# Cross-attention scores of both query tiles of a head pair in one group of twelve 64-row matmuls

## The chip, the core and the metric

The kernel runs on one core of a Trainium2 chip. The metric is the device time of one execution in microseconds (us). TensorE does the matmuls and transposes, VectorE, ScalarE and GpSimd do the elementwise work, each engine takes its own instructions in the order in which they are written, and semaphores order the engines among each other. The DMA queue of SyncE loads the inputs.

## The reference

A cross-attention layer and a mixture-of-experts layer with its own self-attention, in float32. The change touches the cross-attention alone:

```python
# x: (4, 256, 128), ctx: (4, 512, 256); 16 heads of 64
q = split_heads(layernorm(x) @ Wq) * 64 ** -0.5
k, v = split_heads(ctx @ Wkv)                      # 512 keys, and one learned null key and value per head
k = concat(null_k, k); v = concat(null_v, v)
attn = softmax(q @ k.T, axis=-1)
out = layernorm_affine((attn @ v).merge_heads() @ Wout)
x = x + out
x = x + ffn_block(layernorm(x))                    # self-attention, router, 8 experts, top 2
```

## The kernel before

Float32 products are made from three matmuls each: an operand is split into a high part (`_hi`, a ScalarE copy that rounds) and a low part (`_lo`, VectorE's or GpSimd's difference), and hi*hi, hi*lo and lo*hi are summed in PSUM. The functions `..._head` are ScalarE's copies and `..._tail` VectorE's differences.

`cross_attention` (L317) walks over 32 head pairs `g` (4 batches of 8 pairs, two heads of 64 columns each), with one loop `for s in STEPS` per engine (L547 TensorE, L652 ScalarE, L761 VectorE, L846 GpSimd). The order inside each loop body is written out by hand, and it works on several pairs at once: in step s the scores of pairs s+1 and s+2, the transposes of pair s and one of s-1, the value matmuls of s-1 and s, the q projection of s+2, and the keys and values projections of a pair four ahead (only while such a pair is left). 256 queries make two query tiles t of 128.

For one pair g the way is:
- `project_q`: three matmuls into `unit_bank`; `q_head`, `q_tail` give `q_hi`, `q_lo`.
- `scores(g, t)` (L466): for both heads i the 128 queries of tile t against 512 keys. A head has 64 rows, so the two heads use the upper and the lower 64 rows of the array, and their matmuls run as pairs (the trace shows them as x2): six matmuls per tile, L478. There are four score banks; `score_bank(G, i)` gives tile 0 two of them and tile 1 the other two, for every g. Scores wait until the exponentials of the pair before have read the banks (`p_exp`).
- `maximum` (L709) per tile and head, `shift` (L717) makes the bias, `exponential` (L611) per tile and head with its row sum, `null_gap` (L793) and `null_exponential` (L618) for the null key, `whole_sum` (L802), `inverse_sum` (L724), then GpSimd's `normalise` (L809) per tile and head.
- `transpose_probs(g, i, half)` (L493): four 128x128 transposes, of head i, half of the keys, both query tiles, into `t_bank[half]`; there is one bank per half, so a group waits until `probs_tail` of the group two before has read it (`t_lo_s`). `probs_head` (L627) and `probs_tail` (L733) copy out `pT_hi` and `pT_lo`.
- `weighted_values(g, i)` (L512): eight matmuls into `o_part`, half of `out_bank`; `o_copy` (L636) to `o_raw`, `o_halves` (L743) adds the partitions 0-63 and 64-127 of it into `o_sum`, `o_split` (L837, L839) on GpSimd splits it.
- every fourth step `project_out` (L529) multiplies four pairs by `Wout` into `y_part`, the other half of `out_bank`; `y_copy` (L650, even ones) and `y_add` (L759, odd ones) take it out. `weighted_values(s - 1, 1)` of that step waits for this (L509), since both use the one bank.

`unit_bank` is one bank for q, keys, values and context projections in turn: each waits until the one before has been copied out (`keys_head` L585, `keys_tail` L694, `values_copy` L594, `context_head` L601, `context_tail` L701). In a context step two groups of four transposes of the next batch's context (L82) are added, and one step later the keys projection stands behind the transposes. In a null step (s = 9, 17, 25) two transposes of the null probabilities (L544) are added, and `weighted_values(s, 0)` waits for their split.

Of the kernel before, what the change touches and what calls it, by code (L numbers as in the profile page):

```python
# [20 lines left out]
P = 128  # L21
# [5 lines left out]
QT = N // P  # L27
# [46 lines left out]
HP = H // 2  # L74
# [242 lines left out]
def cross_attention(nc, k, dram):  # L317

    with ExitStack() as ctx:
# [39 lines left out]
        AHEAD = HP // 2  # L359
# [65 lines left out]
        def _(pe):  # L425
# [40 lines left out]
            def scores(g, t):  # L466
                if not 0 <= g < NP:
                    return
                G = 2 * g + t
                if t == 0:  # L470
                    pe.wait_ge(q_lo_s, g + 1)
                    if g >= AHEAD:
                        pe.wait_ge(k_lo_s, g - AHEAD + 1)
                if G >= 2:
                    pe.wait_ge(p_exp, 2 * G - 2)
                for m, (q, keys) in enumerate(((q_hi, k.keys_hi), (q_lo, k.keys_hi), (q_hi, k.keys_lo))):
                    for i in range(2):
                        last = pe.matmul(score_bank(G, i)[:, :], q[rows(i), g % 2, t * P:(t + 1) * P], keys[rows(i), g % HP, :],  # L478
                                         start=m == 0, stop=m == 2)
                        if m == 2:  # L480
                            last.then_inc(s_ps, 1)
# [65 lines left out]
            for s in STEPS:  # L547
                transpose_probs(s - 1, 1, 1)
                if not after_context(s):
                    keys_unit(s)  # L550
                scores(s + 1, 1)
# [3 lines left out]
                if after_context(s):  # L555
                    keys_unit(s)
                    weighted_values(s - 1, 1)
                    values_unit(s)
                else:
                    values_unit(s)  # L560
                    weighted_values(s - 1, 1)
                transpose_probs(s, 1, 0)
                project_q(s + 2)
# [3 lines left out]
                scores(s + 2, 0)  # L567
# [3 lines left out]
        def _(act):  # L571
# [80 lines left out]
            for s in STEPS:  # L652
# [3 lines left out]
                exponential(s + 1, 0, 0)  # L656
                probs_head(s, 0, 0)
                probs_head(s, 0, 1)
                exponential(s + 1, 0, 1)
                y_copy(s)  # L660
                if after_context(s):
                    keys_head(s)
                    o_copy(s - 1, 1)
                    values_copy(s)
                else:
                    values_copy(s)
                    o_copy(s - 1, 1)
                null_exponential(s + 1, 0)
# [3 lines left out]
                null_exponential(s + 1, 1)  # L672
                probs_head(s, 1, 0)
                exponential(s + 1, 1, 0)
                exponential(s + 1, 1, 1)
                o_copy(s, 0)
                context_head(s, 1)

        @block.vector
        def _(dve):  # L680
# [80 lines left out]
            for s in STEPS:  # L761
                probs_tail(s - 1, 1, 1)
# [1038 lines left out]
```

## Time and profile before

| | us |
|---|---|
| median of 3 runs (lowest, highest) | 682.86 (681.18, 684.12) |
| the profiled execution | 680.71 |
| its span, first to last instruction | 678.9 |
| TensorE busy | 580.8 (86%) |
| VectorE busy | 512.8 (76%) |
| ScalarE busy | 423.3 (62%) |
| GpSimd busy | 310.9 (46%) |
| cross-attention steps, 53.15 to 321.44 | 268.29, TensorE busy 258.58 |

The busy shares are means over stages that differ. The last row is the part of the span in which the changed loops run in their full form; it begins with the third step. The steps have these lengths, measured between starts of `q_lo` (L687): 8.92 to 8.95 in 18 steps, 10.34 to 10.36 in three, 12.62 in three, 12.84 or 12.85 in three, 7.34 or 7.35 in the last two.

### The profile page before, as it was taken

The numbers are of one execution on the slowest core, as the hardware profiler recorded it, in microseconds if no ns is written. First come the engines' busy times: TensorE is split into PE (matmuls) and PEld (weight loads), VectorE is DVE, ScalarE is ACT, GpSimd is POOL, SyncE is SP. The second block draws the span as 40 slices with busy tenths as digits, with TensorE's granted clock in tenths as the row PEclk, the third lists the DMA queues.
The fourth block names the chain that finished last, engine by engine and source line by source line (L and its number), as shares of the span: only waits on it lengthen the run. The fifth ranks groups of instructions, "written<-read, shape, count | busy, mean of one in ns | idle before, by whom it ended". The sixth has DMA issues, their size and how long they took to land. (4 is left out here: it accounts for less than half of the span.)

```text
span 678.9 us, 11861 instructions
## 1 busy us (share of the span) xinstructions
PE 580.8 (86%) x3500; PEld 457.3 (67%) x3500; DVE 512.8 (76%) x1127; ACT 423.3 (62%) x1030; POOL 310.9 (46%) x555
## 2 busy tenths in 40 slices
PE   2969999998999989999873458999984898788996
PEld 2747777776787768778662355666664786666885
DVE  4657777868678677777955577999954699869995
ACT  3547777767777667877850257888844555444653
POOL 1346667756667656766753547213302504223000
PEclk9979999999999999999986778999987899888999
DMA  7020000001000000000000020000000220200001
GB/s 253 1 56 1 3 30 1 1 2 32 1 1 2 1 0 3 0 1 1 2 1 1 0 90 1 1 1 0 0 1 13 76 74 1 83 0 0 0 0 31
DMA packets 14386, 13.05 MB, mean 19 GB/s; under 512 B 2048, under 2 KB 13696, under 8 KB 14336
## 3 DMA queue, kind: packets, MB, share of 16 engines
q1 hardware_dynamic: 14032, 12.41, 5.7%
q8 instruction: 24, 0.39, 0.2%
q14 instruction: 26, 0.21, 0.1%
q10 hardware_dynamic: 304, 0.03, 0.0%
HBM read 11.92 MB, written 0.52 MB: 18 GB/s over the span
## 5 line engine op out<-in xcount | busy, mean ns | idle before, releaser
L809 POOL TENSOR_SCALAR attn_probs<-attn_probs,rinv 128x512 f32<-128x512 f32 x128 | 87.5, 697 | 23.0 <-DVE rinv L724 22.8
L733 DVE TENSOR_TENSOR pT_lo<-bank,pT_hi 128x512 fp32r<-128x512 f32 x128 | 87.5, 685 | 7.5 <-ACT pT_hi L627 5.5
L709 DVE TENSOR_REDUCE neg_max<-bank 128x1 f32<-128x512 f32 x128 | 82.1, 683 | 11.2 <-PE bank L478 11.2
L611 ACT ACTIVATE attn_probs<-bank,bias 128x512 f32<-128x512 f32 x128 | 87.4, 687 | 4.9 <-DVE bias L717 4.6
L627 ACT ACTIVATE pT_hi<-bank 128x512 fp32r<-128x512 f32 x128 | 73.2, 595 | 14.2 <-PE bank L493 14.0
L493 PE MATMUL bank<-ident,attn_probs 128*128 128x128 f32 x512 | 76.3, 281 | 5.6 <-POOL attn_probs L809 5.3
L493 PEld LDWEIGHTS bank<-ident,attn_probs 128*128 128x128 f32 x512 | 56.6, 142 | 29.0 <-issue 17.8
L1658 ACT ACTIVATE act_hi<-act_f 128x512 fp32r<-128x512 f32 x56 | 35.4, 632 | 57.2 <-DVE act_f L1701 56.9
L512 PE MATMUL bank<-pT_hi,vals 128*128 128x256 f32 x256 | 65.6, 288 | 5.5 <-DVE p0T_lo L750 3.4
L512 PE MATMUL bank<-pT_lo,vals 128*128 128x256 f32 x256 | 64.2, 283 | 0.0
L512 PEld LDWEIGHTS bank<-pT_hi,vals 128*128 128x128 f32 x256 | 48.8, 191 | 8.1 <-issue 4.5
L512 PEld LDWEIGHTS bank<-pT_lo,vals 128*128 128x128 f32 x256 | 48.8, 190 | 1.2
L802 POOL TENSOR_TENSOR total<-row_sum,e 128x2 f32<-128x2 f32 x64 | 14.7, 229 | 74.7 <-ACT e L618 69.9
L1705 DVE TENSOR_TENSOR act_lo<-act_f,act_hi 128x512 fp32r<-128x512 f32 x56 | 44.5, 795 | 2.7 <-ACT act_hi L1658 1.6
L1701 DVE TENSOR_TENSOR act_f<-up_w,gate 128x512 f32<-128x512 f32 x56 | 46.3, 827 | 0.2
L743 DVE TENSOR_TENSOR o_sum<-o_raw 64x256 f32<-64x256 f32 x64 | 27.1, 423 | 23.9 <-ACT o_raw L636 22.8
L1230 ACT ACTIVATE p_raw<-s_pair,neg_max 128x128 f32<-128x128 f32 (+1 forms) x128 | 43.2, 429 | 3.0 <-DVE neg_max L1295 3.0
L1693 DVE TENSOR_TENSOR up_w<-u_bank,wide 128x512 f32<-128x512 f32 x48 | 33.1, 690 | 11.3 <-PE u_bank L1606 9.9
L1518 POOL TENSOR_TENSOR dn_hi<-dn_raw,one 128x896 fp32r<-128x896 f32 x4 | 7.1, 1785 | 69.7 <-PE d_bank L1614 54.1
L1652 ACT ACTIVATE gate<-g_bank 128x512 f32<-128x512 f32 x56 | 32.6, 583 | 8.0 <-PE u_bank L1606 8.0
L829 POOL TENSOR_TENSOR vals<-v_raw,vals 128x512 fp32r<-128x512 f32 x28 | 36.1, 1289 | 2.3
L478 PE MATMUL bank<-keys_hi,q_hi 64*128 64x512 f32 x128 | 32.5, 504 | 5.1 <-DVE q_lo L687 4.8
(273 smaller groups left out, 1658.4 us busy)
## 6 DMA issues: line engine op xcount, KB each, us to landing
ctx_raw<-in_ctx SPq DMA_DIRECT2D x4, 512.0 KB, 4.8
wkv_raw<-in_L_xattn_Wkv SPq DMA_DIRECT2D x2, 1024.0 KB, 10.1
gu_raw<-in_L_ffn_w_gate SPq DMA_DIRECT2D x4, 448.0 KB, 3.6
gu_raw<-in_L_ffn_w_up SPq DMA_DIRECT2D x4, 448.0 KB, 4.3
dn_raw<-in_L_ffn_w_down SPq DMA_DIRECT2D x4, 448.0 KB, 5.2
x<-in_x SPq DMA_DIRECT2D x1, 512.0 KB, 6.4
wq_raw<-in_L_xattn_Wq SPq DMA_DIRECT2D x1, 512.0 KB, 9.8
wout_raw<-in_L_xattn_Wout SPq DMA_DIRECT2D x1, 512.0 KB, 12.1
```

The source lines that it names most:

```text
L493: last = pe.transpose(t_bank[half][:, j * N + t * P:j * N + (t + 1) * P], probs[:, g % 2, i, t, kt * P:(kt + 1) * P], k.ident[:, :])
L512: last = pe.matmul(o_part, k.vals[:, kt, 2 * (g % HP) + i, :], x[:, i, kt, :], start=kt == 0 and n == 0, stop=kt == KT - 1 and n == 1)
L611: act.activation(probs[:, g % 2, i, t, :], score_bank(G, i)[:, :], ACT.Exp, bias=bias[:, t, h:h + 1], scale=X_SCALE, accum_out=row_sum[:, ...
L627: act.activation(pT_hi[:, i, 2 * half:2 * half + 2, :], t_bank[half][:, :].rearrange("p (j n) -> p j n", j=2), ACT.Copy).then_inc(t_hi_s, 1)
L709: dve.tensor_reduce(neg_max[:, t, h:h + 1], score_bank(G, i)[:, :], AX_X, ALU.max, negate=True).then_inc(max_s, 1)
L733: dve.tensor_tensor(pT_lo[:, i, 2 * half:2 * half + 2, :], t_bank[half][:, :].rearrange("p (j n) -> p j n", j=2), f(pT_hi[:, i, 2 * half:2 ...
L809: pool.tensor_scalar(probs[:, g % 2, i, t, :], probs[:, g % 2, i, t, :], rinv[:, t, h:h + 1], 1.0, ALU.mult, ALU.mult).then_inc(p_norm_s, 1)
L829: pool.tensor_tensor(values_of(k, i, t, 1), raw, f(values_of(k, i, t, 0)), ALU.subtract).then_inc(v_lo_s, 1)
L1230: last = act.activation(p_raw[:, p % 4, j, t, 0:n], s_bank[(p % 2) * REP + j][:, t * N:t * N + n], ACT.Exp, bias=neg_max[:, t, REP * (p % ...
L1658: act.activation(act_hi[:, n % 2, :], act_f[:, n % 2, :], ACT.Copy).then_inc(a_hi_s, 1)
L1701: dve.tensor_tensor(act_f[:, n % 2, :], up_w[:, n % 2, :], gate[:, n % 2, :], ALU.mult).then_inc(mul_s, 1)
L1705: dve.tensor_tensor(act_lo[:, n % 2, :], act_f[:, n % 2, :], f(act_hi[:, n % 2, :]), ALU.subtract).then_inc(a_lo_s, 1)
```

## The change

`scores(g, t)` becomes `scores(g)`: both query tiles in one place, at the end of step g-2, twelve matmuls in a row. The waits for free score banks move into its loop over t. Around it the four loop bodies are ordered anew:
- TensorE: `transpose_probs(s, 1, 1)` moves from the next step to directly behind `transpose_probs(s, 1, 0)`; the value matmuls of (s-1, 1) stand ahead of the values projection in every step.
- ScalarE: the four exponentials of a pair come in the order (0,1), (0,0), (1,1), (1,0), with the third ahead of `q_head`; `o_copy(s - 1, 1)` ahead of `values_copy`.
- VectorE: the `o_sum` halves and both reciprocals stand between `probs_tail(s, 1, 0)` and the maxima of the next pair; the second tile's maxima are apart from each other.
- GpSimd: `normalise(s, 0, 0)` moves from the end of the step before into step s, behind the whole sum of tile 1.

```diff
-            def scores(g, t):
+            def scores(g):
...
-                if G >= 2:
-                    pe.wait_ge(p_exp, 2 * G - 2)
-                for m, (q, keys) in enumerate(((q_hi, k.keys_hi), (q_lo, k.keys_hi), (q_hi, k.keys_lo))):
...
+                for t in range(QT):
+                    if g >= 1:
+                        pe.wait_ge(p_exp, 4 * g - 2 + 2 * t)
+                    for m, (q, keys) in enumerate(((q_hi, k.keys_hi), (q_lo, k.keys_hi), (q_hi, k.keys_lo))):
+                        for i in range(2):
+                            last = pe.matmul(score_bank(2 * g + t, i)[:, :], q[rows(i), g % 2, t * P:(t + 1) * P],
+                                             keys[rows(i), g % HP, :], start=m == 0, stop=m == 2)
...
             for s in STEPS:                       # TensorE
-                transpose_probs(s - 1, 1, 1)
                 if not after_context(s):
                     keys_unit(s)
-                scores(s + 1, 1)
                 transpose_probs(s, 0, 0)
                 transpose_probs(s, 0, 1)
                 project_out(s)
                 if after_context(s):
                     keys_unit(s)
-                    weighted_values(s - 1, 1)
-                    values_unit(s)
-                else:
-                    values_unit(s)
-                    weighted_values(s - 1, 1)
+                weighted_values(s - 1, 1)
+                values_unit(s)
                 transpose_probs(s, 1, 0)
+                transpose_probs(s, 1, 1)
                 project_q(s + 2)
                 null_probs(s)
                 context_unit(s, 0)
                 weighted_values(s, 0)
-                scores(s + 2, 0)
+                scores(s + 2)
                 context_unit(s, 1)
...
                 probs_head(s - 1, 1, 1)           # ScalarE
                 if not after_context(s):
                     keys_head(s)
-                exponential(s + 1, 0, 0)
                 probs_head(s, 0, 0)
                 probs_head(s, 0, 1)
                 exponential(s + 1, 0, 1)
+                exponential(s + 1, 0, 0)
+                null_exponential(s + 1, 0)
                 y_copy(s)
                 if after_context(s):
                     keys_head(s)
-                    o_copy(s - 1, 1)
-                    values_copy(s)
-                else:
-                    values_copy(s)
-                    o_copy(s - 1, 1)
-                null_exponential(s + 1, 0)
+                o_copy(s - 1, 1)
+                values_copy(s)
+                exponential(s + 1, 1, 1)
                 q_head(s + 2)
                 null_head(s)
                 context_head(s, 0)
-                null_exponential(s + 1, 1)
                 probs_head(s, 1, 0)
                 exponential(s + 1, 1, 0)
-                exponential(s + 1, 1, 1)
                 o_copy(s, 0)
+                null_exponential(s + 1, 1)
                 context_head(s, 1)
...
                 probs_tail(s - 1, 1, 1)           # VectorE
+                shift(s + 1, 0)
+                maximum(s + 1, 1, 1)
                 if not after_context(s):
                     keys_tail(s)
                 maximum(s + 1, 1, 0)
-                maximum(s + 1, 1, 1)
                 probs_tail(s, 0, 0)
+                probs_tail(s, 0, 1)
                 shift(s + 1, 1)
-                probs_tail(s, 0, 1)
                 y_add(s)
                 if after_context(s):
                     keys_tail(s)
-                o_halves(s - 1, 0)
-                o_halves(s - 1, 1)
                 q_tail(s + 2)
                 null_tail(s)
                 context_tail(s, 0)
+                probs_tail(s, 1, 0)
                 inverse_sum(s + 1, 0)
-                probs_tail(s, 1, 0)
+                o_halves(s - 1, 0)
+                o_halves(s - 1, 1)
+                inverse_sum(s + 1, 1)
                 maximum(s + 2, 0, 0)
                 maximum(s + 2, 0, 1)
-                inverse_sum(s + 1, 1)
-                shift(s + 2, 0)
                 context_tail(s, 1)
...
                 whole_sum(s, 1)                   # GpSimd
+                normalise(s, 0, 0)
                 normalise(s, 1, 0)
                 normalise(s, 1, 1)
+                null_weight(s, 1)
+                null_gap(s + 1, 0)
+                o_split(s - 2)
                 normalise(s, 0, 1)
-                null_gap(s + 1, 0)
-                null_weight(s, 0)
-                o_split(s - 2)
-                null_weight(s, 1)
                 whole_sum(s + 1, 0)
                 null_gap(s + 1, 1)
+                null_weight(s, 0)
                 values_split(s)
-                normalise(s + 1, 0, 0)
```

## Rows read from the trace of the kernel before

**Rows 1.** Busy times in single steps: length, five engines (instructions), granted clock, DMA share, GB/s.
```profile
182.25:192.59 10.34, 10.34 (x74) 8.56 (x73) 7.28 (x16) 7.56 (x22) 6.76 (x15) 1.00 0.01 2
201.51:210.46 8.95, 8.95 (x62) 7.15 (x61) 7.28 (x16) 7.19 (x21) 6.78 (x15) 1.00 0.00 0
219.39:232.01 12.62, 11.73 (x80) 9.73 (x81) 8.03 (x18) 7.60 (x22) 6.75 (x15) 1.00 0.00 0
321.44:328.79 7.35, 6.45 (x50) 5.06 (x49) 6.71 (x16) 5.95 (x17) 6.88 (x14) 1.00 0.01 3
160.47:173.31 12.84, 11.18 (x73) 8.80 (x74) 8.77 (x19) 8.39 (x23) 7.12 (x15) 1.00 0.13 41
```

**Rows 2.** TensorE around a group of six: start, length, engine, line, operands, count.
```profile
213.49 0.40 PE L88 MATMUL bank<-cT_hi,wkv_lo 128*128 128x512 f32 x1
213.82 0.50 PE L478 MATMUL bank<-keys_hi,q_hi 64*128 64x512 f32 x2
...
214.71 1.09 PE L493 MATMUL bank<-ident,attn_probs 128*128 128x128 f32 x8
215.56 0.48 PE L90 MATMUL bank<-wkv_hi,cT_hi 128*128 128x512 f32 x1
```

**Rows 3.** TensorE at the stage's start, twelve score matmuls, then the q projection.
```profile
37.05 0.50 PE L478 MATMUL bank<-keys_hi,q_hi 64*128 64x512 f32 x2 [0.93 <-DVE q_lo L687]
...
38.64 0.39 PE L435 MATMUL bank<-xnT_hi,wq_hi 128*128 128x256 f32 x1
```

**Rows 4.** Timeline of VectorE, a steady step and a late one.
```profile
201.51 0.42 DVE L687 TENSOR_TENSOR q_lo<-bank,q_hi 128x256 fp32r<-128x256 f32 x1 [0.37 <-ACT q_hi L578]
...
202.11 0.69 DVE L733 TENSOR_TENSOR pT_lo<-bank,pT_hi 128x512 fp32r<-128x512 f32 x1
202.99 1.29 DVE L709 TENSOR_REDUCE neg_max<-bank 128x1 f32<-128x512 f32 x2 [0.18 <-PE bank L478]
...
208.10 0.68 DVE L733 TENSOR_TENSOR pT_lo<-bank,pT_hi 128x512 fp32r<-128x512 f32 x1
208.81 0.42 DVE L743 TENSOR_TENSOR o_sum<-o_raw 64x256 f32<-64x256 f32 x1
...
327.85 0.91 DVE L743 TENSOR_TENSOR o_sum<-o_raw 64x256 f32<-64x256 f32 x2
328.79 0.42 DVE L687 TENSOR_TENSOR q_lo<-bank,q_hi 128x256 fp32r<-128x256 f32 x1
```

**Rows 5.** Timeline of ScalarE in the steady steps.
```profile
199.36 0.60 ACT L594 ACTIVATE v_raw<-bank 128x512 f32<-128x512 f32 x1
...
201.10 0.38 ACT L578 ACTIVATE q_hi<-bank 128x256 fp32r<-128x256 f32 x1 [0.32 <-PE bank L435]
...
201.98 0.68 ACT L611 ACTIVATE attn_probs<-bank,bias 128x512 f32<-128x512 f32 x1
...
202.64 0.69 ACT L611 ACTIVATE attn_probs<-bank,bias 128x512 f32<-128x512 f32 x1
...
206.47 1.09 ACT L627 ACTIVATE pT_hi<-bank 128x512 fp32r<-128x512 f32 x2 [0.21 <-PE bank L493]
```

**Rows 6.** TensorE: value matmuls behind transposes up to scores; values projection; q projection.
```profile
161.43 0.36 PE L512 MATMUL bank<-pT_hi,vals 128*128 128x256 f32 x1
...
162.55 0.50 PE L478 MATMUL bank<-keys_hi,q_hi 64*128 64x512 f32 x2
...
197.69 0.47 PE L90 MATMUL bank<-wkv_hi,cT_hi 128*128 128x512 f32 x1
...
200.46 0.36 PE L435 MATMUL bank<-xnT_hi,wq_hi 128*128 128x256 f32 x1
```

**Rows 7.** The output projection's copy in mid-stage, and a wait for it near the end.
```profile
189.06 0.39 ACT L650 ACTIVATE yT<-bank 128x256 f32<-128x256 f32 x1
...
342.90 0.36 PE L512 MATMUL bank<-pT_hi,vals 128*128 128x256 f32 x1 [0.57 <-ACT yT L650]
```

More of the change, by code:

```diff
@@ L464, in context_unit @@
                 project(pe, k, "c", i, 0, unit_bank).then_inc(c_ps, 1)
-            def scores(g, t):
+            def scores(g):
                 if not 0 <= g < NP:
                     return
[L469 to L473, printed above, removed]
-                if G >= 2:
-                    pe.wait_ge(p_exp, 2 * G - 2)
-                for m, (q, keys) in enumerate(((q_hi, k.keys_hi), (q_lo, k.keys_hi), (q_hi, k.keys_lo))):
[L477 to L481, printed above, removed]
+                pe.wait_ge(q_lo_s, g + 1)
+                if g >= AHEAD:
+                    pe.wait_ge(k_lo_s, g - AHEAD + 1)
+                for t in range(QT):
[5 more added lines that the diff above has]
+                                             keys[rows(i), g % HP, :], start=m == 0, stop=m == 2)
+                            if m == 2:
+                                last.then_inc(s_ps, 1)
             def transpose_probs(g, i, half):
```

## The prediction

> **What bounds the kernel now.** I read four views: busy time of the engines in single steps, the timeline of one steady step (TensorE first), the waits of TensorE, and the timelines of VectorE and ScalarE in the same step. The diff touches only the cross-attention stage (36.6 to 359 us), whose loop runs in steps of one head pair; a step is counted here from one `q_lo` subtraction to the next. In a steady step of 8.95 us TensorE is busy for 8.95 us, VectorE for 7.28, ScalarE 7.19, GpSimd 6.78, at full granted clock [rows 1]: TensorE's own queue sets the step. The other kinds: a step with an output projection 10.34 (TensorE busy all of it), one with a projection and the null-key chain 12.62 (busy 11.73), one with a new context 12.84 (busy 11.18), and one with no keys or values left 7.35 (busy 6.45) [rows 1]. Of the steady kind there are 18, of the next three 3 each, of the last 2.
>
> **Edit 1, one group of twelve.** A group of six takes 0.89 us, 213.82 to 214.71, and its entry costs more: 0.33 from the last keys matmul instead of 0.23 [rows 2]. At the stage's start, where both query tiles already run together, twelve take 1.59, 37.05 to 38.64 [rows 3]. So three pairs cost 0.70, and each visit to the 64-row form about 0.2 within the group and 0.1 ahead. One visit per step less: 0.29 less TensorE work. The weights loads are hidden as before. The transposes of (s-1, half 1) join (s, 1, half 0), which saves some 0.04 of first-matmul loss. TensorE's work comes to 8.95 - 0.33 = 8.62 a step, if nothing arrives late.
>
> The Trainium skill (TensorEngine Tiling, Key Properties) says that changing the tiling mode drains TensorE, while another tile of the same mode doesn't. The trace agrees, with 0.33 against 0.23. By that rule alone the change gains 0.3 us a step, about 8 us, and is rival A below.
>
> **Edit 2, VectorE's new order.** The two `o_sum` halves and both reciprocals move between `probs_tail(s,1,0)` and the two maxima, so that ahead of `probs_tail(s,1,1)` more is queued. TensorE now wants that tail early: the transposes (s+1,0,1) write the same bank and come directly behind the keys. I walk the loop from the start of `q_lo` (0).
> - `q_hi` starts at -0.41 and gives ScalarE back after some 0.29, `pT_hi` takes 0.60, so tail (s,1,0) starts at 0.49 (now 0.60 [rows 4, 5]).
> - Tail, maximum and keys tail are 0.69 long but follow each other at 0.60: two maxima take 1.29 [rows 4]. An `o_sum` half does not overlap: it starts 0.71 after a 0.68 tail, two take 0.91, and the next one starts when the second is done (328.79) [rows 4]. So: tail to 1.09, reciprocal 0.18, halves 0.46 + 0.46 = 2.19, reciprocal 0.12, two maxima 1.20: tail (s,1,1) starts at 3.51 and is done at 4.20. Its total is there in time: the last exponential starts at 0.37, done 1.15, then `o_raw`, `e0` and the sum to about 1.8, before 2.19.
> - TensorE: the twelve start at 0.48 and end at 2.07, keys to 3.55, transposes (s+1,0,0) to 3.95. It could go on there, but waits for the tail: 4.26. Four transposes 0.40 (eight take 0.85, 214.71 to 215.56 [rows 2]), eight value matmuls behind transposes 1.02 (161.43 to 162.55 is 1.12 with the entry into scores [rows 6]): values projection at 5.68.
> - The values projection now has nothing behind it to hide the copy to `v_raw`. 197.69 to 199.36 is 1.67 with first-matmul loss, 1.59 without, then 0.60 and 0.05: q projection at 7.92. From there to `q_lo` 1.05 (200.46 to 201.51) [rows 4 to 6]. The loop closes at **8.97**.
>
> So the steady step stays at about 8.95: the 0.33 is paid back as a wait for a tail and an uncovered copy. Bounds: if the halves overlapped like other instructions (0.35 each) no tail is late, and what is left is the round through the copy: from the values projection 2.24 to q, 1.53 to scores, 1.59, keys 1.48, transposes 0.85, values 1.02, together 8.7. With 0.1 more at a joint it is 9.05. I take 8.95, since the `o_sum` rows repeat in every steady step. 18 steps: 0.0 us (-4.5 to +1.8).
>
> The Trainium skill (VectorE: DVE Perf Modes, Two Vector instructions with no wait between them) says that an instruction is held until all earlier ones finished when an input or its output starts in another 32-partition group than that before. `o_sum` reads partitions 0 and 64, and the second half writes from 64. By that rule the reciprocal ahead, the second half and what follows are held. The trace agrees (0.71 and 0.91), and no row shows a half followed by a reciprocal. By the rule the step is 8.97; without it 8.7.
>
> **Edit 3, values matmuls (s-1,1) ahead of the values projection.** They wait until the output projection's result has left the bank they share (`y_first`, `y_whole`). Now the values projection runs meanwhile: the copy at 189.06 is hidden, TensorE has no wait [rows 1, 7]. At the stage's end, where there's no such cover, the same matmuls wait 0.57 [rows 7]. In the new order they always follow directly, and the copy also stands behind two exponentials and a null exponential. From transposes (s,0,1) at 4.26: `pT_hi` 0.69 later (4.95), 0.49, exponentials 0.66 each (201.98 to 202.64) [rows 5], 0.11, copy 0.39: 7.25; value matmuls 7.3, 0.95, values projection at 8.25, plus 2.24 and 1.05: 11.55 against 10.34, **+1.2** in 3 steps: +3.6. In the three null steps VectorE's `y_add` is last, behind keys tail, a maximum, two tails and a shift: keys at 3.60 after `q_lo` (the null chain holds scores until 2.0), `keys_lo` from 5.90, `y_add` 8.39 to 8.81, TensorE ready at 8.04: 13.15 against 12.62: **+0.5** each, +1.5. With nothing ahead of them the copies would cost the 0.57 alone, less the 0.33: +0.25 each, 1.5 in all six; that is the lower bound.
>
> **The rest.**
> - Context steps: context transposes and `cT` copies stay, keys wait for `cT_lo` behind both halves and maxima: 12.73 against 12.84, -0.3 for three (-1.2 to +0.5).
> - The two steps without keys and values: nothing covers VectorE's row of tails. Tail (0,1) ends at 6.68, last transposes 6.74, q 7.10, `q_lo` 8.18 against 7.35: **+1.7** for two (0 to +2.5).
> - Start: `exponential(0,1,1)` now precedes `q_head(1)`: +0.66, and keys and values follow without scores between: +1.0 (0.5 to 1.5).
> - Normalise (s,0,0) moves behind the whole sum into step s. GpSimd has norm (s,1,0) done at 3.2 and TensorE needs it at 3.55: nothing. The four norms ahead of transposes (s,1,.) end at 6.5, needed at 7.0. `exponential(s+1,1,0)` is done at 1.15, wanted by the seventh matmul at 1.28: nothing, but 0.1 late would be paid fully. End of the stage: norms and copies move both ways, 0 (-1 to +1). DMAs, other stages: untouched.
>
> **Sum.** 0 + 3.6 + 1.5 - 0.3 + 1.7 + 1.0 = **+7.5 us**. The profiled execution took 680.7 us (span 678.9), so 688.2; the median of the three runs is 682.9, so the forecast is 690.4. A measurement of this kernel tells about 0.5% (3.4 us) from no change.
>
> **Rivals.**
> A. *Faster: TensorE stays the bound.* If tails and copies arrive in time, 27 steps save 0.3, less the start: -7, 676. For it: TensorE is busy all of a steady step, and the others have 1.7 us left. Against: that slack isn't where the new order needs it (4.20 against 3.95), and the bank's wait in projection steps follows from the code. From a steady step under 8.75 and no wait ahead of the values matmuls it decides. Chance 0.15.
> B. *Only the projection steps lose.* Steady steps 8.7, thus -4.5 from the sum: +3.0, 686. For it: the missing row for half and reciprocal. Chance 0.27.
> C. *More is late.* ScalarE's `q_head` now stands behind an exponential, the second six scores behind the last exponential; 0.1 to 0.15 lost at these joints in each of 27 steps: +4, 694.5. Against: each has 0.1 left by rows. Chance 0.13.
> The forecast has 0.45: TensorE's gain taken by VectorE's order.
>
> **How the numbers follow.** Slower by over 0.5% (above 686.3): forecast and C, and a little of B: 0.60. Same: most of B: 0.23. Faster: A and a tail of B: 0.17. The range reaches from the lower part of B, with some of the tail steps' loss gone, to C: 681 to 695.5.
>
> **What would show it.** Right: twelve score matmuls in about 1.6 us and one visit per step; steady steps of 8.8 to 9.0 with a TensorE wait for `pT_lo` of 0.2 to 0.3 ahead of transposes (s,0,1), a small one for `v_raw` ahead of q; waits of about 1 us for `yT` ahead of value matmuls in projection steps; last steps over 8 us. Wrong: steady steps of 8.7 or less, `o_sum` followed by a reciprocal in less than 0.4, or no `yT` wait. A longer wait on GpSimd's norms would mean that I placed its queue wrongly.

## The result: slower, by more than the forecast range held

The changed kernel takes 699.3 us (698.0 to 703.5 in 4 runs), the kernel before 682.0 beside it (680.5 to 684.1): a ratio of 1.026, interval [1.021, 1.032]. The forecast was 690.4 with 681 to 695.5 as its range, so the direction is right and the loss of 17.3 us is more than twice the 7.5 foreseen. The profiled execution took 703.5 us, its span is 701.7 against 678.9. The engines' totals on the page after:

```profile
PE 584.6 (83%) x3500; PEld 464.0 (66%) x3500; DVE 508.7 (72%) x1127; ACT 418.8 (60%) x1030; POOL 316.3 (45%) x555
...
L801 POOL TENSOR_SCALAR attn_probs<-attn_probs,rinv 128x512 f32<-128x512 f32 x128 | 93.3, 739 | 0.1
```

Instruction counts are as before, and all four busy shares fell: the kernel mostly waits more. Two engines are busy a little longer. GpSimd's 5.4 us more are those of `normalise` (739 ns on average against 697; more on that at the end), and TensorE's 3.8 more come from the part behind the changed stage (255.4 to 260.6, below), where its clock was lower in this execution. Single steps of the kernel after, columns as in [rows 1], in the order steady, with an output projection, with a new context, with the null-key chain, one of the last two; then from the last `q_lo` to the end of the stage, and the rest of the kernel:

```profile
208.62:217.62 9.00, 8.90 (x62) 7.21 (x61) 7.12 (x16) 7.05 (x20) 7.04 (x15) 1.00 0.00 0
187.85:199.60 11.75, 10.58 (x74) 8.70 (x73) 7.13 (x17) 7.45 (x21) 7.05 (x15) 1.00 0.00 0
164.58:178.86 14.28, 11.08 (x73) 8.80 (x74) 8.42 (x18) 8.28 (x22) 7.00 (x15) 1.00 0.13 38
226.63:239.93 13.30, 11.56 (x80) 9.93 (x81) 7.83 (x18) 7.39 (x21) 6.67 (x15) 1.00 0.00 0
341.50:349.81 8.31, 6.28 (x50) 4.99 (x49) 6.53 (x15) 5.94 (x18) 5.05 (x12) 1.00 0.01 2
349.81:379.75 29.94, 20.32 (x124) 17.70 (x123) 14.17 (x31) 11.75 (x31) 11.80 (x25) 0.82 0.00 1
379.75:701.70 321.95, 260.60 (x1420) 201.63 (x1418) 253.28 (x562) 175.87 (x397) 90.18 (x102) 0.87 0.06 20
```

The last two stretches in the kernel before:

```profile
336.13:364.21 28.08, 20.32 (x127) 17.14 (x126) 13.69 (x30) 12.89 (x33) 11.84 (x26) 0.88 0.00 1
364.21:678.90 314.69, 255.44 (x1420) 198.18 (x1418) 251.92 (x562) 175.67 (x397) 90.17 (x102) 0.90 0.06 20
```

Together these give the 22.8 us between the two profiled spans (mean length of each kind of step, after less before):

| part | forecast | measured |
|---|---|---|
| stage start, first `q_lo` to that of the first steady step | +1.0 | +0.8 (16.58 to 17.37) |
| 18 steady steps | 0.0 | +0.8 (8.94 to 8.98) |
| 3 with a projection | +3.6 | +4.1 (10.35 to 11.73) |
| 3 with the null chain | +1.5 | +1.9 (12.62 to 13.27) |
| 3 with a new context | -0.3 | **+4.3** (12.84 to 14.28) |
| last two | +1.7 | +1.9 (7.35 to 8.32) |
| end of the stage | 0 | **+1.9** (28.08 to 29.94) |
| cross-attention in all (it starts 0.2 earlier) | +7.5 | +15.5 |
| rest of the kernel, not changed | 0 | +7.3, of this one execution |

The last line is not the change's work. The same 1420 matmuls take 314.7 us at a mean granted clock of 0.90 and 322.0 at 0.87. Over the thirteen profiles of this study that part takes 314.6 to 315.3 at 0.90 (four of them), 317 to 317.5 at 0.89 (seven), 318.7 at 0.88 and 322.0 at 0.87. It doesn't follow the change: the kernel b_q2 below, whose stage ends at 374.3 us, has 314.6, and a_ctx, at 376.2, has 318.7. Of the 17.3 us between the medians it is some 1.8 if the stage takes 15.5 in all runs, and more if the end of the stage is mostly shorter than in this one (see further below). That is why steps, not totals, are compared below.

**A steady step after**, in the timeline (TensorE at the start of each group, and what VectorE and ScalarE do between):

```profile
208.62 0.42 DVE L679 TENSOR_TENSOR q_lo<-bank,q_hi 128x256 fp32r<-128x256 f32 x1 [1.70 <-ACT q_hi L573]
209.10 0.50 PE L477 MATMUL bank<-keys_hi,q_hi 64*128 64x512 f32 x2
209.90 0.87 DVE L735 TENSOR_TENSOR o_sum<-o_raw 64x256 f32<-64x256 f32 x2
210.69 0.50 PE L88 MATMUL bank<-cT_hi,wkv_hi 128*128 128x512 f32 x1
210.81 0.17 DVE L716 RECIPROCAL rinv<-total 128x2 f32<-128x2 f32 x1
...
212.07 0.68 DVE L725 TENSOR_TENSOR pT_lo<-bank,pT_hi 128x512 fp32r<-128x512 f32 x1
...
212.87 0.42 PEld L492 LDWEIGHTS bank<-ident,attn_probs 128*128 128x128 f32 x4 [0.31 <-POOL attn_probs L801]
...
214.32 0.40 PE L90 MATMUL bank<-wkv_hi,cT_hi 128*128 128x512 f32 x1
...
215.90 0.60 ACT L589 ACTIVATE v_raw<-bank 128x512 f32<-128x512 f32 x1
216.55 0.39 PE L435 MATMUL bank<-xnT_hi,wq_hi 128*128 128x256 f32 x1
```

From `q_lo`: twelve scores 1.59 long, tail at +3.45 (forecast 3.51), values projection at +5.70 (5.68), q at +7.93 (7.92), next `q_lo` at +9.00 (8.97). The wait at 212.87 carries GpSimd's name, since its third normalise ended last by the profile, but the first four transposes needed the same normalises and had gone through; what the second four need is the tail, done at 212.75.

The copy to `v_raw`, of which the forecast said that nothing hides it any more, costs next to nothing: q starts 0.86 after the eight transposes began, and eight take 0.85 in [rows 2], ahead of a values projection that waits for nothing. So the step's loss is the wait for the tail alone. The kernel after has a control of its own for this: the first steady step has no `o_sum` halves yet (there is no pair before the first), and it takes 8.72, with the same 62 matmuls and TensorE never waiting. GpSimd has less to do in it too; a_halves below tests the halves alone.

```profile
53.70:62.42 8.72, 8.72 (x62) 7.23 (x61) 6.27 (x14) 6.89 (x20) 5.58 (x13) 1.00 0.00 1
```

**A context step and a projection step**, same view (the last two rows are of the projection step):

```profile
169.94 0.66 PE L492 MATMUL bank<-ident,attn_probs 128*128 128x128 f32 x4 [0.78 <-POOL attn_probs L801]
170.04 0.68 DVE L693 TENSOR_TENSOR cT_lo<-bank,cT_hi 128x512 fp32r<-128x512 f32 x1
...
170.64 0.68 DVE L725 TENSOR_TENSOR pT_lo<-bank,pT_hi 128x512 fp32r<-128x512 f32 x1
...
171.47 0.63 PE L492 MATMUL bank<-ident,attn_probs 128*128 128x128 f32 x4 [0.86 <-DVE pT_lo L725]
171.85 0.48 PE L88 MATMUL bank<-cT_hi,wkv_hi 128*128 128x512 f32 x1
...
174.04 0.60 ACT L580 ACTIVATE keys_hi<-bank 128x512 fp32r<-128x512 f32 x1
...
175.42 0.50 PE L90 MATMUL bank<-wkv_hi,cT_hi 128*128 128x512 f32 x1 [0.99 <-DVE keys_lo L686]
...
194.72 0.39 ACT L645 ACTIVATE yT<-bank 128x256 f32<-128x256 f32 x1
...
195.25 0.36 PE L511 MATMUL bank<-pT_hi,vals 128*128 128x256 f32 x1 [1.06 <-ACT yT L645]
```

The same two places in a context step of the kernel before:

```profile
165.81 1.27 PE L493 MATMUL bank<-ident,attn_probs 128*128 128x128 f32 x8 [0.38 <-POOL attn_probs L809]
...
169.89 0.50 PE L90 MATMUL bank<-wkv_hi,cT_hi 128*128 128x512 f32 x1 [0.46 <-DVE keys_lo L694]
```

TensorE waits 1.06 us for `yT` in the projection step, where [rows 7] had no wait at 189.06. In the context step it waits 0.86 for a tail, where it had no wait, 0.99 for `keys_lo` instead of 0.46, and 0.78 for GpSimd's norms instead of 0.38; a wait of 0.25 for `v_raw` is gone. The forecast had none of the three that grew. All five repeat in every step of their kind (waits of the kernel after, 60 to 335 us: total, times, longest):

```profile
PE bank L511 <- ACT yT L645: 3.2, 3, 1.1
...
PE bank L90 <- DVE keys_lo L686: 3.0, 3, 1.0
PE bank L492 <- DVE pT_lo L725: 2.6, 3, 0.9
PE bank L511 <- DVE yT L751: 2.5, 3, 0.8
PE bank L492 <- POOL attn_probs L801: 2.3, 3, 0.8
```

**In the last two steps** it is GpSimd's norms that TensorE waits for, and not the row of tails of the forecast. One of the two, and then the longest wait in the same step of the kernel before:

```profile
336.62 0.66 PE L492 MATMUL bank<-ident,attn_probs 128*128 128x128 f32 x4 [1.28 <-POOL attn_probs L801]
337.46 0.63 PE L492 MATMUL bank<-ident,attn_probs 128*128 128x128 f32 x4 [0.19 <-DVE pT_lo L725]
...
339.60 0.66 PE L492 MATMUL bank<-ident,attn_probs 128*128 128x128 f32 x4 [0.55 <-POOL attn_probs L801]
```
```profile
325.13 0.66 PE L493 MATMUL bank<-ident,attn_probs 128*128 128x128 f32 x4 [0.77 <-POOL attn_probs L809]
```

### The profile page after: what moved, and what is told of

Read it like the earlier page. It is cut to its first block and busy times, and to the rows that moved or that the text cites. A ratio compares the mean times of both kernels' runs of the same rounds, so it can differ in the third digit from the quotient of the medians.

```text
span 701.7 us, 11861 instructions
## 1 busy us (share of the span) xinstructions
PE 584.6 (83%) x3500; PEld 464.0 (66%) x3500; DVE 508.7 (72%) x1127; ACT 418.8 (60%) x1030; POOL 316.3 (45%) x555
## 5 line engine op out<-in xcount | busy, mean ns | idle before, releaser
L801 POOL TENSOR_SCALAR attn_probs<-attn_probs,rinv 128x512 f32<-128x512 f32 x128 | 93.3, 739 | 0.1
L725 DVE TENSOR_TENSOR pT_lo<-bank,pT_hi 128x512 fp32r<-128x512 f32 x128 | 84.7, 680 | 10.3 <-ACT pT_hi L622 8.7
L492 PE MATMUL bank<-ident,attn_probs 128*128 128x128 f32 x512 | 73.5, 279 | 15.5 <-POOL attn_probs L801 10.0
L622 ACT ACTIVATE pT_hi<-bank 128x512 fp32r<-128x512 f32 x128 | 76.2, 600 | 16.0 <-PE bank L492 14.2
L492 PEld LDWEIGHTS bank<-ident,attn_probs 128*128 128x128 f32 x512 | 59.7, 143 | 30.9 <-POOL attn_probs L801 25.0
L511 PE MATMUL bank<-pT_hi,vals 128*128 128x256 f32 x256 | 67.9, 297 | 11.8 <-ACT yT L645 4.2
L679 DVE TENSOR_TENSOR q_lo<-bank,q_hi 128x256 fp32r<-128x256 f32 x32 | 13.6, 424 | 75.2 <-ACT q_hi L573 75.2
L1693 DVE TENSOR_TENSOR act_f<-up_w,gate 128x512 f32<-128x512 f32 x56 | 47.9, 855 | 0.2
L580 ACT ACTIVATE keys_hi<-bank 128x512 fp32r<-128x512 f32 x28 | 16.7, 598 | 49.2 <-PE bank L88 49.2
L1606 PE MATMUL d_bank<-act_hi,dn_hi 128*128 128x512 f32 x56 | 24.2, 433 | 17.3 <-DVE act_lo L1697 17.3
```

The lines of the kernel that those rows point to most:

```text
L492: last = pe.transpose(t_bank[half][:, j * N + t * P:j * N + (t + 1) * P], probs[:, g % 2, i, t, kt * P:(kt + 1) * P], k.ident[:, :])
L511: last = pe.matmul(o_part, k.vals[:, kt, 2 * (g % HP) + i, :], x[:, i, kt, :], start=kt == 0 and n == 0, stop=kt == KT - 1 and n == 1)
L622: act.activation(pT_hi[:, i, 2 * half:2 * half + 2, :], t_bank[half][:, :].rearrange("p (j n) -> p j n", j=2), ACT.Copy).then_inc(t_hi_s, 1)
L725: dve.tensor_tensor(pT_lo[:, i, 2 * half:2 * half + 2, :], t_bank[half][:, :].rearrange("p (j n) -> p j n", j=2), f(pT_hi[:, i, 2 * half:2 ...
L801: pool.tensor_scalar(probs[:, g % 2, i, t, :], probs[:, g % 2, i, t, :], rinv[:, t, h:h + 1], 1.0, ALU.mult, ALU.mult).then_inc(p_norm_s, 1)
L1606: last = pe.matmul(d_bank[c][:, :], w[:, slot, s, :], x[:, n % 2, :], start=False, stop=False)
```

## Experiments

Theory 1 is the forecast's: TensorE bounds the kernel before, grouping saves it 0.2 to 0.3 us a step, and the new orders around it cost more. The rivals: the grouping itself costs, or TensorE's work isn't the bound. Steps are means of a kind, as in the table above; ratios are to the kernel before.

**a_halves** (kernel after): the `o_sum` halves in their old place.
```diff
+                o_halves(s - 1, 0)
+                o_halves(s - 1, 1)
                 q_tail(s + 2)
...
                 inverse_sum(s + 1, 0)
-                o_halves(s - 1, 0)
-                o_halves(s - 1, 1)
                 inverse_sum(s + 1, 1)
```


> The changed kernel with VectorE's two o_sum halves put back ahead of q_tail, where it idles for 1.7 us in a steady step. Theory 1 (the halves hold back the tail (s,1,1) that the transposes (s+1,0,1) wait for): steady steps fall from 9.00 to 8.7, bound by the uncovered copy v_raw; the last two steps fall by 0.3 or more; the stage loses 5 to 7 us. Rival (TensorE waits there for something else, such as GpSimd's norms): steady steps stay at 9.0 and the wait changes its name. Projection steps keep their wait for yT of about 1 us under both.

Steady 8.98 to 8.71, 688.2 us, 1.008 [1.005, 1.011]. A steady step of it has TensorE busy throughout:

```profile
205.66:214.38 8.72, 8.72 (x62) 7.23 (x61) 7.15 (x16) 6.88 (x20) 6.98 (x15) 1.00 0.00 0
```

So two instructions of 0.87 us together, in front of the late tail, ate TensorE's whole gain. The last two steps fall by 0.35 each (8.32 to 7.97), as expected, and the projection steps keep their wait for `yT` (1.14 to 1.17). The end of the stage falls to 28.13.

Where the gain of 0.23 comes from can be read from the same two steady steps (201.51 before, 205.66 here), from the start of one group to that of the next. The scores take 1.59 instead of 0.91 and 0.90, the keys projection 1.50 instead of 1.57, the values projection 1.40 instead of 1.47, together 0.36 less. The two groups of value matmuls, of which one now stands directly behind transposes, take 2.14 instead of 2.04, and transposes with the q projection 2.10 instead of 2.06. The 0.04 that the forecast expected of the joined transposes didn't come.

**a_values** (after): in projection and null steps the values projection goes first again, and ScalarE's `values_copy` ahead of its `o_copy` alike.
```diff
-                weighted_values(s - 1, 1)
-                values_unit(s)
+                if projected_at(s) is not None:
+                    values_unit(s)
+                    weighted_values(s - 1, 1)
+                else:
+                    weighted_values(s - 1, 1)
+                    values_unit(s)
```


> The changed kernel, where in the eight projection steps alone the values projection stands ahead of the value matmuls (s-1,1) again, and values_copy ahead of o_copy. Theory 1 (the wait for the shared bank costs its full length): even projection steps fall from 11.74 to about 10.5, null steps from 13.3 to about 12.7, together 5 to 6 us less. Rival (other queues are as late there, the wait only covers them): less than 2 us, with a new wait behind the values projection. Steady steps stay at 9.0.

Projection 11.73 to 10.35, null 13.27 to 12.32, steady unchanged at 8.98; 690.3 us, 1.014 [1.007, 1.020]. The uncovered copy to `yT` is the cause in both kinds, and mending it gives 7.0 us, more than the 5 to 6 expected.

**a_ctx** (after): `probs_tail(s, 1, 1)` ahead of `cT_hi(1)`, `cT_lo(1)` (both copies), and after a context `keys_head` ahead of the second exponential.
```diff
-                probs_head(s - 1, 1, 1)           # ScalarE
...
                 exponential(s + 1, 0, 1)
+                if after_context(s):
+                    keys_head(s)
                 exponential(s + 1, 0, 0)
                 null_exponential(s + 1, 0)
                 y_copy(s)
-                if after_context(s):
-                    keys_head(s)
...
+                probs_head(s, 1, 1)
                 context_head(s, 1)
...
-                probs_tail(s - 1, 1, 1)           # VectorE
...
+                probs_tail(s, 1, 1)
                 context_tail(s, 1)
```


> The changed kernel with the order around the second context copy mended: probs_head(s,1,1) and probs_tail(s,1,1) ahead of context_head(s,1) and context_tail(s,1), and in the step after it keys_head between the two exponentials instead of behind them. Theory 1 (context steps lose 1.4 us because the tail stands behind the context copy, 0.86 us of wait at TensorE, and the keys copy behind two exponentials, 0.5 us): the three context steps fall from 14.28 to about 13.0, 3 to 4 us in all, nothing else moves. Rival (the wait for GpSimd's norms ahead of it, 0.78, is what counts and the rest follows): less than 1 us.

Context steps 14.28 to 13.36: 0.92 of the 1.44 lost; 696.1 us, 1.021 [1.016, 1.026]. The wait for the tail falls from 0.86 to 0.27 and that for `keys_lo` from 0.99 to 0.47, its length before the change: both came from places in queues. Less than the expected 13.0, since the rival has a part: the wait for the norms stays at 0.78, 0.40 more than before the change. In a_halves it is 0.49 and in a_all below 0.50, where the tail's wait is gone as well, and the context step takes 12.89.

**b_q2** (kernel before): the three q matmuls twice, the same result.
```diff
-                for i, (w, x) in enumerate(((k.wq_hi, k.xnT_hi), (k.wq_hi, k.xnT_lo), (k.wq_lo, k.xnT_hi))):
+                for i, (w, x) in enumerate(((k.wq_hi, k.xnT_hi), (k.wq_hi, k.xnT_lo), (k.wq_lo, k.xnT_hi)) * 2):
...
-                                     start=i == 0, stop=i == 2)
+                                     start=i % 3 == 0, stop=i % 3 == 2)
```


> The kernel before with each q projection done twice (three more 128x256 matmuls a step, 0.35 us of TensorE; the first result is overwritten). Theory 1 (TensorE bounds every step of the kernel before): steady steps rise from 8.95 to 9.30, 32 steps bring 10 to 11 us. Rival (other queues had slack inside a step that would absorb it): less than 5. Second question: if the stages behind cross-attention only shift, the total rises by the stage's difference; if their clock depends on when they start, the total moves by 1 to 8 us more or less than the stage.

Steady +0.356 (8.936 to 9.292), as much as the added work; 691.7 us, 1.016 [1.010, 1.022]. The other kinds rise by 0.35 to 0.36 too, the last two by 0.30: the added work lies on the path in every kind, also where TensorE has waits. The q projection stands on the round from q through `q_lo` to the scores as well as in TensorE's queue, so this run alone doesn't tell the two apart; b_visit adds its work elsewhere. The stages behind only shift: they take 314.6 here and 314.7 before.

**b_visit** (before): the six scores of (s+1, 1) in two visits, four ahead of and two behind transposes (s,0,0). The new third argument picks the pairs of matmuls that a visit does.
```diff
-                scores(s + 1, 1)
+                scores(s + 1, 1, (0, 1))
                 transpose_probs(s, 0, 0)
+                scores(s + 1, 1, (2,))
```


> The kernel before with the third pair of the scores of tile 1 put behind the first four transposes of (s,0): the same instructions, but one visit more to the 64-row form per step. It prices a visit alone. Theory 1 (each visit costs TensorE 0.3): steady steps 9.2 to 9.3, total +8 to +10 us. Rival (a visit costs only its 0.1 at the entry, the rest is the first matmul behind transposes): 9.05, total +3.

```profile
207.22:216.50 9.28, 9.28 (x62) 7.10 (x61) 7.36 (x16) 7.26 (x21) 6.73 (x15) 1.00 0.00 0
```

The same 62 records, TensorE never waiting, 0.34 us more a step (692.6 us, 1.013 [1.010, 1.016]). A visit to the 64-row form costs 0.34 by itself, in a kernel whose steady step TensorE's work fills; taking one away gave 0.23 (8.936 to 8.71), as read above under a_halves. The last two steps rise by 0.95 each here, which wasn't looked into.

**b_twelve** and **b_twelve_exp** (before): the second six move behind the first; then `exponential(s+1,1,0)` too goes ahead, next to `values_copy`.
```diff
-                scores(s + 1, 1)
...
                 scores(s + 2, 0)
+                scores(s + 2, 1)
```


> The kernel before with the grouping alone: scores(s+1,1) moves to directly behind scores(s+1,0), all other orders kept. Theory 1 (grouping saves 0.3 us of TensorE per step, but the second six then wait for the last exponential, done 1.8 us after q_lo where they could start at 1.3): steady steps about 9.1 to 9.2, with a wait of 0.5 for attn_probs inside the twelve; total +3 to +8 us. Rival (the order of the others is not needed for it): steady steps 8.65, total -8.

> The same, and one more edit: exponential(s+1,1,0) moves ahead of q_head, between values_copy and o_copy, where ScalarE idles 0.35 us and waits 0.3 for q. Values projection and transposes stay where they were in the kernel before. Theory 1 (the loss lies in the new order, not in the group of twelve): steady steps 8.66, projection, null and context steps 0.2 to 0.3 shorter than before too, 7 to 8 us less than before in all. Rival (the group itself brings queues together that collide, whatever the order): steady steps 8.9 or more, no gain.

A miss in both. The wait of 0.50 for `attn_probs` inside the twelve came as expected in b_twelve, and moving the exponential takes it down to 0.11 or less, but one of 0.54 for `keys_lo`, which neither expectation had, came with it in both. Steady steps 10.15 and 9.70 instead of 9.1 to 9.2 and 8.7; 712.6 us, 1.045 [1.042, 1.048], and 698.1, 1.023 [1.021, 1.025]. Steady step of b_twelve_exp:

```profile
204.65 0.60 ACT L627 ACTIVATE pT_hi<-bank 128x512 fp32r<-128x512 f32 x1 [1.37 <-PE bank L493]
...
205.84 1.04 PE L493 MATMUL bank<-ident,attn_probs 128*128 128x128 f32 x8
206.04 0.60 ACT L585 ACTIVATE keys_hi<-bank 128x512 fp32r<-128x512 f32 x1 [0.80 <-PE bank L88]
...
206.68 0.69 DVE L695 TENSOR_TENSOR keys_lo<-bank,keys_hi 128x512 fp32r<-128x512 f32 x1 [0.71 <-ACT keys_hi L585]
...
207.42 0.53 PE L90 MATMUL bank<-wkv_hi,cT_hi 128*128 128x512 f32 x1 [0.54 <-DVE keys_lo L695]
```

Keys end at 206.0, two copies (0.60, 0.69) must empty `unit_bank` before the values projection, and only transposes stand between. The six scores had stood there: they covered those copies. In the kernel after, the value matmuls of (s-1, 1) fill that gap. So the rival is half right: grouping alone costs, through the cover it takes from a bank with one tenant at a time. Some new order is needed, and a_halves and a_all show one that keeps the gain.

**a_lower** (after): both `o_sum` halves read and write only lower partitions (0 to 63), the second into a tile of its own. This leaves out the sum over the two partition halves and the second head's part of `o_sum`; the places in the queue stay.
```diff
-        o_sum = sb("o_sum", [P, 2, N])
+        o_sum, o_other = sb("o_sum", [P, 2, N]), sb("o_other", [P, 1, N])
...
-                dve.tensor_tensor(o_sum[rows(i), g % 2, :], o_raw[0:DH, g % 2, i, :], o_raw[DH:P, g % 2, i, :], ALU.add).then_inc(o_sum_s, 1)
+                dve.tensor_tensor((o_sum[0:DH, g % 2, :], o_other[0:DH, 0, :])[i], o_raw[0:DH, g % 2, i, :], o_raw[0:DH, g % 2, i, :], ALU.add).then_inc(o_sum_s, 1)
...
+            pool.memset(o_sum[:, :, :], 0.0)
```


> The changed kernel with both o_sum adds kept to partitions 0 to 63: each adds the lower half of o_raw to itself and writes partitions 0 to 63, the second into a tile of its own (the upper heads' values are left out, so the output isn't the reference's). Same count, size and places. Theory 1 (VectorE holds an instruction whose inputs or output start in another 32-partition group than the last): halves follow each other in 0.35 instead of 0.46 and the reciprocals around them too, tail (s,1,1) comes 0.3 earlier, steady steps fall from 9.0 to 8.7, 5 us in all. Rival (sources in SBUF make it slow whatever the partitions): pace 0.46, steady steps 9.0.

```profile
208.01 0.15 DVE L716 RECIPROCAL rinv<-total 128x2 f32<-128x2 f32 x1
208.09 0.40 DVE L735 TENSOR_TENSOR o_sum<-o_raw 64x256 f32<-64x256 f32 x1
208.41 0.41 DVE L735 TENSOR_TENSOR o_other<-o_raw 64x256 f32<-64x256 f32 x1
```

Reciprocal to half 0.08 instead of 0.18, half to half 0.32 instead of 0.46: no longer held, in the same place. Steady steps 8.80 (693.5 us, 1.019 [1.016, 1.023]), 0.18 of the expected 0.3, as the second reciprocal now waits for its total: it starts at 208.91, and GpSimd's sum ends at 208.88. The edit also makes both inputs the same slice, so it shows that the pace depends on where these operands lie, and not which of the two inputs or the output does it. By the Trainium skill (VectorE: DVE Perf Modes, Two Vector instructions with no wait between them) these instructions are held because inputs and outputs start in different 32-partition groups; the trace agrees. By that rule it is the first half that waits for the reciprocal ahead of it, and not the reciprocal, as the forecast had it; its figures are the same either way.

**b_halves** (before): the halves behind `probs_tail(s, 1, 0)`, as in the kernel after, nothing grouped.
```diff
-                o_halves(s - 1, 0)
-                o_halves(s - 1, 1)
                 q_tail(s + 2)
...
                 probs_tail(s, 1, 0)
+                o_halves(s - 1, 0)
+                o_halves(s - 1, 1)
                 maximum(s + 2, 0, 0)
```


> The kernel before with VectorE's two o_sum halves moved to behind probs_tail(s,1,0), ahead of the two maxima, as the change has them; TensorE's order unchanged. Theory 1 (the halves cost only because TensorE's new order wants the tail (s,1,1) directly behind the keys): in the old order that tail is wanted over 1 us later and VectorE idles 0.7 us ahead of it, so steady steps stay within 0.1 of 8.94, total +0 to +3. Rival (the halves in this place cost by themselves): 9.2, total +5.

A miss: steady 9.66, neither 9.04 at most nor the rival's 9.2; 706.0 us, 1.037 [1.033, 1.040].

```profile
212.17 1.29 POOL L829 TENSOR_TENSOR vals<-v_raw,vals 128x512 fp32r<-128x512 f32 x1
...
213.05 1.52 DVE L743 TENSOR_TENSOR o_sum<-o_raw 64x256 f32<-64x256 f32 x2
213.44 0.87 POOL L809 TENSOR_SCALAR attn_probs<-attn_probs,rinv 128x512 f32<-128x512 f32 x1
...
215.81 0.15 DVE L724 RECIPROCAL rinv<-total 128x2 f32<-128x2 f32 x1
...
216.82 0.55 PE L493 MATMUL bank<-ident,attn_probs 128*128 128x128 f32 x3 [0.74 <-POOL attn_probs L809]
```

The halves take 1.52 beside GpSimd's work, and here the second reciprocal stands behind them, so the norms that transposes (s+1,0,0) need start at 216.07. The first steady step, without halves, takes 8.93. Which of the two costs most wasn't separated. An estimate from these rows: with halves of 0.87 the reciprocal would come 0.65 earlier, nearly the whole wait of 0.74 at 216.82.

**a_all** (after): a_halves, a_values and a_ctx together, and in steps without keys and values the q projection ahead of `transpose_probs(s, 1, 1)`.
```diff
-                transpose_probs(s, 1, 1)
-                project_q(s + 2)
+                if unit_at(s) is None:
+                    project_q(s + 2)
+                    transpose_probs(s, 1, 1)
+                else:
+                    transpose_probs(s, 1, 1)
+                    project_q(s + 2)
```


> The changed kernel with four mends together: halves ahead of q_tail, values projection first in projection steps, tail and keys copy mended around the second context copy, and in steps without keys and values the q projection ahead of transposes (s,1,1). If the losses are separate and add up: steady 8.71, even projection steps 10.1 to 10.35, null 12.3, context 13.1, last 7.4; the stage ends 2 to 4 us earlier than before, total 678 to 682. If they share a cause, the stage stays above the kernel before.

**Faster than the kernel before**, by 0.7%: 678.4 us against 682.8, 0.993 [0.990, 0.995]. The stage ends 2.3 us earlier in the profiled executions (361.9 against 364.2). Steps: 8.71, 10.06 to 10.42 (projection), 12.31, 12.89, 7.90. The losses are separate, but for the last two steps: 7.4 was expected there, and TensorE still waits 1.06 and 0.54 for GpSimd's norms. One steady and one projection step:

```profile
200.44:209.13 8.69, 8.69 (x62) 7.22 (x61) 7.15 (x17) 6.85 (x20) 7.01 (x15) 1.00 0.00 0
181.68:191.74 10.06, 10.06 (x74) 8.58 (x73) 7.11 (x17) 7.33 (x21) 7.89 (x15) 1.00 0.01 2
```

**a_best** (a_all): at the stage's start `q_head` goes ahead of `exponential(0,1,1)`; in the last steps `normalise(s+1,0,0)` goes back to the end of the step before.
```diff
-                exponential(s + 1, 1, 1)
+                if s >= 0:
+                    exponential(s + 1, 1, 1)
                 q_head(s + 2)
+                if s < 0:
+                    exponential(s + 1, 1, 1)
...
                 whole_sum(s, 1)
-                normalise(s, 0, 0)
+                if unit_at(s - 1) is not None:
+                    normalise(s, 0, 0)
...
                 values_split(s)
+                if unit_at(s) is None:
+                    normalise(s + 1, 0, 0)
```


> The changed kernel with all four mends, and two more at the ends: before step 0 q_head ahead of the third exponential, and normalise(s,0,0) back at the end of the step before where no values are left. Steady 8.71, even 10.1, null 12.3, context 12.9 as with the four; start 17.2 instead of 17.8, last steps 7.5 instead of 7.9: 1 to 1.5 us less than with the four, 676 to 678. If the last steps stay at 7.9, GpSimd's norm isn't what TensorE waits for there.

678.6 us, 0.996 [0.993, 0.998]: 0.4% faster than the kernel before, not told apart from a_all. The start is 1.0 shorter (17.80 to 16.81); the last steps are 7.90 and 8.28, no better: TensorE waits 1.07 and 1.10 for GpSimd's norms, and in the second of them 0.42 for a tail. So the place of that one normalise isn't what makes the norms late.

## Why the forecast was right in sign and wrong in size

- *Bound and saving (edit 1).* Right: b_q2 and b_visit show TensorE as the bound of the steady step, twelve scores take the forecast 1.59. The saving, forecast 0.33, is 0.23 (a_halves): the value matmuls behind transposes give 0.10 of it back.
- *Steady steps (edit 2), 0.0.* Right, mechanism and size (+0.8 in 18): the walk meets the joints named above within 0.06 us, and a_halves gives the 8.7 of rival B. The place of the halves costs 0.27 a step (8.98 to 8.71), and a_lower takes back 0.18 of it in the same place by no longer holding them. One part of the forecast's reason is wrong: "an uncovered copy" costs nothing that can be seen, and the small wait for `v_raw` that it gave as a sign isn't there; the tail's wait is the whole loss.
- *Projection and null steps (edit 3), +3.6 and +1.5.* Right mechanism (a_values), an eighth and a quarter too small.
- *Context steps, -0.3 for three: this step failed, and it is the largest error, 4.6 us.* It had the keys projection wait for `cT_lo`; the keys don't wait at all (171.85). What waits is ahead of them: the transposes (s+1,0,1) now need `probs_tail(s,1,1)`, and that stands behind `cT_lo(1)`: 0.86. `keys_head` stands behind a second exponential and a null exponential: it starts at 174.04, 0.56 after the keys projection's end (before the change 0.04, at 168.51), and the values projection, with all eight value matmuls through, waits 0.99 for `keys_lo`, 0.53 more than before. The wait for GpSimd's norms grows by 0.40, where the forecast took "nothing". Less the 0.25 for `v_raw` that is gone, these make 1.54 us of added waits; with 0.10 less work they are the 1.44 that the step is longer. a_ctx mends 0.92 of 1.44, and with the halves moved too (a_all) all but 0.05.
- *End of the stage, 0 (-1 to +1): failed too.* +1.9 (29.94), at a mean granted clock of 0.82 against 0.88. In a_halves it is 28.13 at 0.88. But a_values and a_ctx keep the late halves, ran here at 0.88, and have 28.54 and 28.79. So the order costs 0.5 to 0.7 here, and the other 1.2 to 1.4 go with the clock of that one execution. Why it was lower stays open.
- *Start, +1.0.* Right (+0.8), and a_best takes 1.0 off by putting `q_head` first again.
- *Last two, +1.7.* The size is right (+1.9), largely by luck: the forecast had VectorE's tails as the reason, and they make TensorE wait 0.19. The rest is GpSimd's norms, 1.28 and 0.55 in each step against one wait of 0.77 or 0.58 before.
- *The rest of the kernel* was taken as fixed; it moves with its granted clock by up to 7 us from one profiled execution to another.
- *Rivals.* Rival A asked for steady steps under 8.75 and no `yT` wait: neither came, but a_all meets both and is faster. Rival B's steady step is a_halves. Rival C has the nearest time, not the mechanism: its joints cost nothing in steady steps.
- Of the signs listed as wrong for the forecast the first three didn't show. The last one did, in the context steps (0.78 against 0.38) and the last two: GpSimd's queue was placed wrongly there. The range was too narrow, since the kinds of step not walked had bounds of a few tenths each.

## What to carry over

When work is grouped to save a bounding engine's time, ask of each block that moves what it had covered: here six score matmuls hid two copies out of a shared bank, and taking them away cost 0.76 us a step (b_twelve_exp, 0.54 of it in one wait), where the grouping can give 0.23. Walk every kind of step through the new queues, the rare ones first: nine special steps of 32 made 10.4 of 15.5 us here. And when a regrouping fails, mend each neighbour that it moved by itself: four such places mended turned a ratio of 1.026 into 0.993.

## What the runs showed of the hardware

- VectorE and GpSimd slow each other. In the kernel after, each half keeps its 0.42 to 0.46, and the normalise that runs beside the second takes 0.92 instead of 0.69 (27 of 128 do, which makes the mean 739 ns, 697 before). In b_halves the halves are stretched too: 0.69 beside the end of the values split and 0.81 beside a normalise of 0.87, 1.52 in all. In a_lower, where the halves end before the norms start, all 128 take 0.68 to 0.70. Beside `pT_lo`, which has one input in PSUM, a normalise keeps 0.69 (211.98 in the kernel after). By the Trainium skill (GPSIMD Engine Reference, Specifications) their SBUF interfaces are shared, with contention for VectorE instructions with two SBUF inputs, which `o_sum` has; the trace agrees.
- A visit to the 64-row form costs 0.34 us when added (b_visit). When one is removed, 0.36 goes from the scores and the two projections, and 0.14 comes back in the value matmuls, of which one group then follows transposes directly, and in the transposes with the q projection (a_halves).
- Two 64x256 halves that start on other partitions than the instruction before follow each other at 0.46, those that don't at 0.32 (a_lower).
